# Edge rows loaded for 64 partitions and ten apart, and two comparisons of a search placed one and two chunks later

## The reference

```python
h   = maximum(layernorm(x), 0)
att = sigmoid(h[src] @ W_att[:128] + h[dst] @ W_att[128:] + b_att)
agg = segment_sum((h[src] @ W_msg + b_msg) * att, dst)
gi  = agg @ W_ih.T + b_ih;  gh = h @ W_hh.T + b_hh        # three gates each
r, z = sigmoid(i_r + h_r), sigmoid(i_z + h_z)
n   = tanh(i_n + r * h_n)
h_new = (1 - z) * n + z * h
out = x + gamma * (h_new - mean) * rsqrt(var + 1e-5) + beta   # mean, var over the nodes
```

## Time and profile before

| | |
|---|---|
| median of 3 runs | 2293.05 us (2293.02 to 2302.7) |
| the profiled execution's own time | 2292.99 us |
| its span, first to last instruction | 2291.2 us |
| busy: PE, DVE, ACT, POOL | 2046.7, 1991.6, 2033.7, 1682.9 us |
| mean granted TensorE clock | 0.966 |
| DMA, mean over the span | 75 GB/s |

### The profile page before, as it was taken

One profiled execution on the slowest core, in us unless ns is written; L12 is line 12 of the kernel. 1 busy time (PEld: TensorE's weight loads), 2 busy tenths in 40 slices (PEclk: granted clock), 3 DMA queues, 4 the chain that ended last, 5 costly groups with the idle time before them and its releaser, 6 DMA issues.

```text
span 2291.2 us, 53895 instructions
## 1 busy us (share of the span) xinstructions
PE 2046.7 (89%) x18152; PEld 1984.0 (87%) x18152; DVE 1991.6 (87%) x4337; ACT 2033.7 (89%) x7078; POOL 1682.9 (73%) x1601
## 2 busy tenths in 40 slices
PE   1434899999999999999999999999999999999995
PEld 1433799999999999999999999999999999999995
DVE  2665899999999999999999999999999999999973
ACT  1667999999999999999999999999999999999933
POOL 4477777777777777777777777777777777777760
PEclk9865799999999999999999999999999999999997
DMA  6683222222222222222222222222222222222236
GB/s 108 182 221 94 53 60 57 63 59 62 60 62 60 64 60 61 61 62 59 64 61 62 61 62 60 62 61 61 60 61 62 60 62 60 63 59 64 58 92 236
DMA packets 171127, 171.66 MB, mean 75 GB/s; under 512 B 82824, under 2 KB 135098, under 8 KB 170722
## 3 DMA queue, kind: packets, MB, share of 16 engines
q0 software_dynamic: 50688, 104.63, 20.6%
q1 hardware_dynamic: 114564, 61.63, 10.3%
q10 hardware_dynamic: 5598, 1.93, 0.7%
HBM read 141.39 MB, written 26.66 MB: 73 GB/s over the span
## 4 chain that ended last, share of the span: by engine, by line
ACT 48%; PE 22%; DVE 11%; issue 7%; POOL 3%; DMA 2%; SPq 1%; DVEq 0%; ACTq 0%; POOLq 0%
ACT big L922 38%; PE ps L1462 12%; ACT gate_ring L918 9%; DVE big L1213 5%; PE ps L1447 4%; PE ps L1457 3%; POOL big L777 2%; DVE gate_ring L1197 2%; DMA row_ring<-node_table,set_idx 1%; DVE key_hot L1183 1%; PE ps L1468 1%; POOL row_ring L786 1%; PE ps L1469 1%; DVE lo_hot L1176 1%; ACT n_blk L927 1%
## 5 line engine op out<-in xcount | busy, mean ns | idle before, releaser
L786 POOL DMA_INDIRECT row_ring<-node_table,set_idx x1480 | 1573.3, 1063 | 462.0 <-issue 332.8
L922 ACT ACTIVATE big<-set_score,big 128x128 f32<-128x128 f32 x5096 | 1631.9, 393 | 78.4 <-PE ps L1462 78.4
L1462 PE MATMUL ps<-big 128*128 128x128 f32 x10192 | 1445.9, 281 | 0.0
L1462 PEld LDWEIGHTS ps<-big 128*128 128x128 f32 x10192 | 1262.2, 192 | 0.0
L1213 DVE TENSOR_TENSOR big<-ps,big 128x784 f32<-128x784 f32 x832 | 803.8, 966 | 4.7 <-PE ps L1457 3.5
L1447 PE MATMUL ps<-gate_ring,row_ring 128*128 128x64 f32 x2960 | 536.0, 263 | 75.4 <-DVE gate_ring L1197 69.7
L1447 PEld LDWEIGHTS ps<-gate_ring,row_ring 128*128 128x128 f32 x2960 | 453.2, 194 | 123.7 <-DVE gate_ring L1197 109.2
L1197 DVE SCALAR_TENSOR_TENSOR gate_ring<-lane,set_rel,gate_ring 128x64 f32<-128x64 f32 x1480 | 415.5, 281 | 136.5 <-ACT gate_ring L918 131.5
L918 ACT ACTIVATE gate_ring<-set_win,row_ring 128x64 f32<-128x64 f32 x1480 | 492.0, 340 | 35.9 <-DMA row_ring<-node_table,set_idx 31.6
L1457 PE MATMUL ps<-key_hot,lo_hot 128*128 128x196 bf16 x3328 | 426.2, 251 | 24.1 <-DVE key_hot L1183 19.7
L1183 DVE TENSOR_TENSOR key_hot<-lane_key,set_key 128x1568 bf16<-128x1568 bf16 x416 | 402.9, 968 | 0.0
(11 more groups left out here) (125 smaller groups left out, 960.8 us busy)
## 6 DMA issues: line engine op xcount, KB each, us to landing
row_ring<-node_table,set_idx POOLq DMA_INDIRECT x1480
big<-in_x_dram SPq DMA_DIRECT2D x48, 256.0 KB, 4.2
h_blk<-hT_spill SPq DMA_DIRECT2D x97, 64.0 KB
node_table<-big SPq DMA_DIRECT2D x24, 258.0 KB
hT_spill<-big SPq DMA_DIRECT2D x24, 256.0 KB, 5.3
out_dram<-big SPq DMA_DIRECT2D x24, 256.0 KB
set_win<-dst_scores SPq DMA_DIRECT2D x148, 32.0 KB
set_score<-dst_scores SPq DMA_DIRECT2D x52, 64.0 KB, 3.0
```

The lines of the kernel that those rows point to most:

```text
L786: nc.gpsimd.indirect_dma_start(row_ring[:, t % ROWS_RING, :], None, table, bass.IndirectOffsetOnAxis(ap=set_idx[:, t // SET % 2, t % SET:t ...
L922: return nc.scalar.activation(a_buf[b % 2][:, h, :], set_score[:, b % 2, :], ACT.Sigmoid, bias=m_all[:, h, D:ROW])
L1462: return nc.tensor.matmul(ps[:, AM_BANK, 0:P], m_all[:, h, 0:D], a_buf[b % 2][:, h, :], start=h == 0, stop=h == HI - 1)
```

## The change

The two DMAs of line 883 become four. Each is cut by partition: rows 0 to 63 (`GROWS - GROWS % 16`), and rows 64 to 73. The same bytes land in the same places. The two waits on `sparse_loaded` go from 32 to 64. And `find_firsts` runs at c = 16 and c = 20 of DVE's program instead of 15 and 18.

```diff
                 if c == 1:
                     for rows, edges in ((src_rows, src), (dst_rows, dst)):
-                        act.dma_start(rows.bitcast(I32).rearrange("g (c e) -> g c e", c=2),
-                                      edges[0:GROUPS * GEDGES].rearrange("(c g e) -> g c e", c=2, e=GEDGES)
-                                      ).then_inc(sparse_loaded, 16)
+                        for part_of in (slice(0, GROWS - GROWS % 16), slice(GROWS - GROWS % 16, GROWS)):
+                            act.dma_start(rows.bitcast(I32).rearrange("g (c e) -> g c e", c=2)[part_of, :, :],
+                                          edges[0:GROUPS * GEDGES].rearrange("(c g e) -> g c e", c=2, e=GEDGES)[part_of, :, :]
+                                          ).then_inc(sparse_loaded, 16)
...
                 if c == 5:
-                    act.wait_ge(sparse_loaded, 32)
+                    act.wait_ge(sparse_loaded, 64)
...
             def sparse_windows():
-                dve.wait_ge(sparse_loaded, 32)
+                dve.wait_ge(sparse_loaded, 64)
...
-                if c in (15, 18):
-                    find_firsts((c - 15) // 3)
+                if c in (16, 20):
+                    find_firsts((c - 16) // 4)
```

## The result

Five runs of the changed kernel gave 2278.57 us (2274.15 to 2280.91) against 2296.6 us for the kernel before beside it; the ratio is 0.9928, 95% interval 0.9913 to 0.9943, that is 16.5 us less (13 to 20). (The ratios here are not exactly the quotients of the two medians: those differ by 18.0 us.) The profiled execution took 2278.57 us, span 2276.8: 14.4 us less than the profiled one of before (2292.99). The forecast was 24 us less. The time lies outside the forecast's own range of 2265 to 2274 us and at the upper end of the wider one of 2262 to 2279. The direction, the place and the chain were right; the size was not.

A forecast was written before the change was run, and what follows sets the result against it. The main loop waits for POOL's gathers, stalled 30.3 us behind `find_tiles`, held late by edge rows on two engines. First row gather at 162.6 instead of 186.88, 24.3 us earlier, gives 2269 us; own range 2265 to 2274, wider 2262 to 2279.

The forecast's parts named there:

- chunk 2 (`x` landed): DVE's statistics of chunk 2, at 22.54 before, come at 24.5, 2 us allowed for edge rows standing before its `x`.
- chunk 2 to `sparse_windows`, four steps: DVE's chunks 2 to 5 in stage A: four pipeline steps of 3.5 us, 14.0 us in all, to 38.5.
- T: When DVE begins chunk 6, 69.97 us before: forecast 43.7, bounds 40.5 and 48.4.
- `firsts_found` 0, from T: DVE's comparison for half 0, moved to chunk 16: T + 44.8 plus one step of 3.2 us, at 91.7.
- first window to first row gather: POOL's stretch from first window gather to first row gather stays 70.8 us, contention included.
- first row gather, moved by: POOL issues the first table-row gather at 162.6 instead of 186.88 us, 24.3 us earlier.
- 3.9 us for the edge rows on sixteen engines: The split loads' 296 packets at 0.21 us, 62 us of engine time, take 3.9 us over 16 DMA engines.
- the second rival: DMA engines take over: steps stretch to 5 us, chunk 2 at 28, T 53.2, time 2278.2 us; chance 13%.
- the ten issues of ACT at c = 4: ACT's ten issues of 0.45 us delay its next Relu by some 3 us, so 3.5 us a step was taken.
- the step of the pipeline, 3.2 us: Undisturbed time per chunk step in stage A, 3.2 us; `find_firsts` at chunk 16 comes one such step later.
- POOL without a gap: Rival: DVE early enough (T under 39) that POOL never waits; gain 29.2 us, 2263.8 us; chance 18%.
- the loads bring nothing: Rival: split loads drain no faster, T stays, the moved comparison makes POOL wait 1.9 us, 2294.9 us; chance 7%.

The follow-up runs named there:

- The loads alone: The changed kernel with `find_firsts` back at chunks 15 and 18, the split loads kept: 2271.71 us, ratio 0.9907 to the kernel before.
- the loads by themselves: A kernel without the layer that only loads edges, each case waited for, and writes zeros: 74 partitions 16.9 us, 64 with 10 partitions 6.65 us.
- the changed kernel again: The changed kernel unaltered, run and profiled a second time: 2276.69 us, ratio 0.9930 to the kernel before.

## Why the prediction was right in kind and too large

The profiled executions, by the forecast's own steps:

| step | forecast | changed kernel | earned or lost |
|---|---|---|---|
| chunk 2 (`x` landed) | 24.5 | 24.78 | |
| chunk 2 to `sparse_windows`, four steps | 14.0 | 19.74 | 5.7 lost |
| T, chunk 6 | 43.7 | 49.83 | 6.1 lost in all |
| `tiles_found` 0 | T + 11.2 | T + 11.4 | 0.2, not on the path |
| `firsts_found` 0, from T | T + 48.0 | T + 51.9 | 3.9 lost |
| from `firsts_found` to the first window gather | 0.1 | 0.8 | 0.7 lost |
| first window to first row gather | 70.8 | 70.5 | 0.3 earned |
| first row gather, moved by | 24.3 | 13.9 | 10.4 lost |

**What held.** What the path is: POOL's queue, its stall behind `find_tiles`, and behind that the edge rows on two engines. The loads alone bring 21.7 us of the time (2293.36 to 2271.71) with one edit, and the earlier trace rows had 0.21 us a packet, which the loads by themselves repeat. The blocked issues behind the loads vanished (18.84 to 0.60 us for the small load). ACT stayed ahead of the first row, as forecast. The rule of the Trainium skill against cutting a transfer (DMA: Bandwidth & Descriptors, section Rules for kernel authors) did not apply: the uncut one is the one that takes 17 us alone, the cut one 6.65.

**The step that failed first** is the term of 14.0 us for four steps of the pipeline, chunks 2 to 5, and with it that of 3.9 us for the edge rows on sixteen engines. The four steps took 19.74 us, which is 5.7 of the 6.1 us that T came late; in the two other profiles of the same code (the changed kernel again, the loads alone) they took 19.12 and 19.06, although chunk 3 waited for `x` in one and not in the other. For the edge rows I multiplied packets by a duration measured on two engines. Alone it is 0.34 us a packet on sixteen, in the kernel about 0.40 with 11 us for the whole, and chunk 3, for which I had allowed no wait, waited 7.83 us.

But the experiments with later loads show that this wait is not lost one for one: with it moved away, T and the time stay. Nor is T by itself what the path goes through: with `sparse_windows` moved behind, chunk 6 came 6.3 us earlier and chunk 7 at the same time. What the steps follow is the loop over the landing of `hT_spill`, of which my sum had no term of its own; with its store issued first the time fell by about 6 us. All of the traffic is in this stretch: the DMA share of the second profile of the changed kernel, here 20 to 60 us, is at or near 1, against the 0.58 of the earlier trace rows:

```profile
20.00:30.00 10.00, 2.85 (x12) 2.55 (x12) 1.48 (x10) 2.89 (x7) 7.59 (x8) 1.00 1.05 169
30.00:40.00 10.00, 2.85 (x12) 2.54 (x12) 4.14 (x24) 4.22 (x11) 7.56 (x9) 1.00 0.91 193
40.00:50.00 10.00, 2.28 (x16) 2.10 (x17) 8.43 (x47) 3.10 (x7) 7.56 (x9) 0.81 0.95 202
50.00:60.00 10.00, 5.94 (x32) 5.49 (x31) 5.53 (x16) 6.66 (x14) 2.51 (x3) 0.67 0.97 192
```

That the full engines are why the store lands late is argued from this and not shown: in the earlier trace rows the share is 0.97 from 120 to 140 us too, where I counted steps of 3.2 to 3.4 us. I had this as the second rival, at 2278.2 us, with 13%. Its steps of 5 us are what came (4.9). Its chunk 2 at 28 and its T of 53.2 did not come, and that its time is nearly the measured one is in part luck: a T 3.4 us too late made up for a comparison counted 3.9 us too early. A smaller part of the same term: the ten issues of ACT at c = 4, which I had at 4.5 us, took 7.6 us (38.85 to 46.44), and the next Relu waited 5.66 us behind them.

**The second** is the step of the pipeline, 3.2 us. That was an average over eight steps that are far from alike, and it says little of the one to which `find_firsts` was moved. In the kernel before the comparison came 4.8 us later by it. With the loads alone `firsts_found` came at T + 44.8, exactly as the forecast had it for chunk 15, and 6.7 us behind the statistics of that chunk. In the changed kernel it came 13.4 us behind them and, in the second profile, 10.1: the one chunk more took 6.7 and 3.5 us. By the times the move cost 5 us and not 2.7, and 3.4 instead of 1.9 in the kernel before.

**The rivals.** POOL without a gap did not come: the waits sum to 13.5 us. That the loads bring nothing is ruled out by 21.7 us. The main loop moved with its first gate (2102.2 us from there to the end, 2103.5 before); over the profiled executions of this study on the chips of about 2293 us it lies between 2101.9 and 2108.8 us, which is more than the differences between several of these versions.

## What to carry to other kernels

Look at how many engines a load really uses: bytes, packets and share of its queue in a quiet window show it at once. Here 74 partitions ran on about two engines, and the cut into 64 and 10 was worth 21.7 us; no other count without a factor of 16 was tried, but for 10 alone (2.8 us). When the load is spread, expect its rate to grow by less than its engines (alone, the cut load took 6.65 us for 16.9, 2.5 times faster with 8 times the engines for most of it), and expect what stood idle behind it to crowd into the gap. Before a piece of work is added to a sum of a path, look whether it is hidden in a wait of something else: taking `sparse_windows` out from in front of `find_tiles` won nothing. A step that is handed back and forth between two engines should be placed by the waits it leaves in both, and placed again after every change that moves one of them: here the placing that came with the loads gave back a quarter of what they brought.

## What the runs showed of the hardware that I had not expected

- The time of a packet of 5120 bytes, with no other traffic: 0.21 us when two engines work (49 GB/s together, 740 KB in 15 us), 0.34 when sixteen fill 64 partitions, 0.25 when sixteen fill 128. The lower and the upper half of the partitions are alike (5.8 and 5.4 us from issue to the end of the wait, 5.5 and 5.5 in the second round), and the same bytes into 32 partitions take no longer (5.0). Why was not tried further.
- The same program took 2293 us on the other chips and 2648 on one, with every version slower alike and with other waits on the path.
